# Opening laid out anew, and sum, squares and halves of two chunks moved to GpSimd

## Chip, cores and metric

One core of a Trainium2 chip. The metric is the device time of one execution, in microseconds. Engines by the names of the profile: PE is TensorE, DVE is VectorE, ACT is ScalarE, POOL is GpSimd, SP is the queue that issues most transfers.

## The reference

A conditioned transformer block on x of 8 batches by 256 tokens by 128 channels:

- condition: `sc = silu(c)`, `shift = sc @ shift_w.T + shift_b`, `scale = clip(sc @ scale_w.T + scale_b + 1, 0.1, 10)`
- `adaln(x) = x / max(norm(x) / sqrt(128), 1e-6) * norm_w * scale + shift`
- attention with 16 heads of 8 channels: softmax of `q k / sqrt(8)` with the keys whose mask value is 0 left out (a batch with no valid key gets equal weights), then times v, then the projection; `x = x + attention(adaln(x))`
- MLP: 128 to 1024 channels, halves `x1` and `x2`, `silu(x1) * x2`, 512 to 128; `x = x + mlp(adaln(x))`

## The kernel before

Channels lie on the partitions and tokens run along the row. The 2048 tokens are four chunks of 512 (two batches each). In the opening they come in five pieces (`PIECES`): pieces 0 and 1 are the two batches of chunk 0, pieces 2 to 4 are chunks 1 to 3.

**Opening, for each piece e.** ACT squares x (`square`), PE averages over the channels with a matmul against `mean_w` (`mean_square`), ACT takes a logarithm and an exponential (`inverse_norm`), DVE multiplies (`norm`), ACT applies gain and shift (`shifted`) and gives `h`. PE makes queries, keys and values from `h` (`q_or_k`, `values`). Queries and keys are cut into three bf16 parts: the first by ACT (`first_part_q`, `first_part_k`), the remainder by DVE (`rest_of_q`, `rest_of_k`), the rest by POOL (for piece 0 by DVE). Transfers lay the parts row by row into `q_stack` and `k_stack`, with rows for the mask and for the maxima.

**Attention.** A unit is a pair of heads of one batch, 64 units in all. The loop on PE runs over positions p = 0 to 71. At position p, PE makes the scores of unit p with queries on the partitions (`query_scores`, two banks of a ring of three), and of unit p - 8 with keys on the partitions (`key_scores`, another ring of three); at u = p - 8 it also multiplies exponentials by values (`p_times_v`). DVE takes the maxima of the first kind of scores, two reductions of a unit (`maxima`). After each four units (half a batch, index k) POOL cuts the maxima in two bf16 parts, PE turns them (`turn_maxima`, position 4k + 4), DVE copies them (`turned`) and POOL issues two transfers that put them into `q_stack`. ACT takes the exponentials of the second kind of scores. The ring of three banks holds scores, turned maxima, the projected chunk and its mean square in one order (`ITEMS`); a bank is written again once its last user has read it, and every engine works in program order.

**Between.** SP stores the outputs with their sums to DRAM and loads them back as `o_num` and `o_den`. When a chunk is complete, at fixed positions behind it (`P_...`), ACT takes the reciprocal of the sums, DVE multiplies (`over_sum`), PE projects (`project`), DVE adds x (`residual`), ACT squares (`square_2`), PE averages (`mean_square_2`), DVE applies the lower bound (`guard_2`), ACT makes the inverse norm, DVE multiplies in two halves (`norm_2`), ACT adds the shift and rounds to `h2_hi` (`shifted_2`), DVE makes the remainder `h2_lo` (`second_part_h2`). This is so for chunks 0 and 1; chunks 2 and 3 end in the MLP loop. Three times two instructions of POOL cut the MLP weights between k = 6 and k = 11 (L463, L466).

**MLP.** 16 steps of two three-part matmuls, a sigmoid, two multiplications and a three-part matmul back.

Positions that the change touches: `PRE_...` are positions p at which pieces 2 to 4 do their steps (PE: `PRE_SQUARE`, `PRE_Q`, `PRE_K`, `PRE_V`; DVE: `PRE_NORM`, `PRE_REST_Q`, `PRE_REST_K`). POOL works its loop over k at L429 to L466. The order on ACT in the opening is written out at L806 to L840, on PE at L686 to L697, on DVE at L1089 to L1106.

## Time and profile before

| | us |
|---|---|
| median of 3 runs | 187.12 |
| lowest, highest run | 186.57, 262.2 |
| profiled execution | 188.25 |
| its span, first to last instruction | 186.2 |

| engine | busy us | share of the span |
|---|---|---|
| PE | 150.3 | 81% |
| DVE | 147.9 | 79% |
| ACT | 136.3 | 73% |
| POOL | 75.5 | 41% |

The profiled execution's own time is 2.05 us more than its span. Sums below are made against the profiled execution. All times inside the trace are in us from the span's start. A line number such as L1032 is the line of the kernel that issued the instruction.

### The profile page before, as it was taken

To read this page: it belongs to the slowest core of one execution; us is meant where nothing else is said; L and a number is where in the kernel's file an instruction comes from. 1 tells how busy PE (TensorE), PEld (TensorE's weight loads), DVE (VectorE), ACT (ScalarE), POOL (GpSimd) and SP (SyncE) were. 2 spreads that over 40 slices of the span, in tenths; PEclk is the share of its full clock that TensorE was granted. 3 is DMA by queue.
4 is the path that set the end of the run, shared out by engine and by line. 5 is a ranking of instruction groups with operands and counts; after the bars stand their busy time and mean duration, and the time that the engine had idled before them with its cause. 6 is when DMAs were issued, how large, how long until landed. Compare 5 with 4: busy or idle time off the path is not lost.

```text
span 186.2 us, 3731 instructions
## 1 busy us (share of the span) xinstructions
PE 150.3 (81%) x1312; PEld 75.8 (41%) x1312; DVE 147.9 (79%) x258; ACT 136.3 (73%) x247; POOL 75.5 (41%) x125
## 2 busy tenths in 40 slices
PE   7772997649998898778867778877799994998992
PEld 7440543323333333223323322323223872785870
DVE  8675389875999999998999998999332956987993
ACT  7566265666778888957978856988988699689550
POOL 8249117975663133603423512302300252553750
PEclk9997599996999999999999999999999999999999
DMA  4846224427311373621112112112122110010103
GB/s 131 277 145 204 78 80 138 127 58 206 90 59 61 118 206 110 192 89 40 58 60 58 62 60 58 56 59 61 62 84 85 65 51 0 2 56 0 55 5 113
DMA packets 17512, 16.38 MB, mean 88 GB/s; under 512 B 2846, under 2 KB 16598, under 8 KB 17494
## 3 DMA queue, kind: packets, MB, share of 16 engines
q1 hardware_dynamic: 16086, 15.21, 26.5%
q0 software_dynamic: 1408, 0.93, 1.9%
q8 instruction: 11, 0.18, 0.4%
q14 instruction: 7, 0.06, 0.1%
HBM read 4.34 MB, written 5.24 MB: 51 GB/s over the span
## 4 chain that ended last, share of the span: by engine, by line
DVE 35%; PE 28%; issue 15%; DMA 7%; POOL 7%; SPq 3%; ACT 3%; DVEq 0%; POOLq 0%; ACTq 0%
DVE neg_max L1032 24%; PE bank L549 5%; POOL gated_lo L473 5%; PE bank L619 3%; PE bank L511 3%; ACT p_exp L882 2%; DMA mask_sb<-mask 2%; PE bank L601 2%; DMA o_rows<-o_sb 2%; PE bank L521 2%; PE bank L570 2%; DVE o_num L1053 2%; PE bank L575 2%; DMA o_den<-o_rows 2%; SPq L318 2%
## 5 line engine op out<-in xcount | busy, mean ns | idle before, releaser
L1032 DVE TENSOR_REDUCE neg_max<-bank 128x2 f32<-128x512 f32 x128 | 81.8, 686 | 12.0 <-PE bank L549 11.4
L882 ACT ACTIVATE p_exp<-bank 128x512 f32<-128x512 f32 x128 | 69.5, 598 | 20.5 <-PE bank L601 19.5
L619 PE MATMUL bank<-p_exp,v_all 128*9 128x256 f32 x512 | 40.0, 386 | 0.2
L549 PE MATMUL bank<-k_stack,q_stack 62*128 62x256 bf16 x256 | 26.3, 281 | 17.0 <-DVE neg_max L1032 11.7
L473 POOL TENSOR_TENSOR gated_lo<-rs,gated_hi 128x512 fp32r<-128x512 f32 x14 | 18.2, 1302 | 28.6 <-ACT gated_hi L906 27.6
L601 PE MATMUL bank<-q_stack,k_stack 64*128 64x256 bf16 x256 | 25.9, 274 | 3.9 <-DVE rest L997 2.0
L549 PEld LDWEIGHTS bank<-k_stack,q_stack 62*128 62x128 bf16 x256 | 8.9, 94 | 45.5 <-DVE neg_max L1032 36.1
L445 POOL DMA_DIRECT2D q_stack<-max_rows x32 | 17.6, 553 | 20.8 <-DVE max_rows L1041 20.8
L435 POOL CAST max_parts<-neg_max 128x16 bf16<-128x16 f32 x16 | 3.5, 220 | 47.2 <-DVE neg_max L1032 47.2
L601 PEld LDWEIGHTS bank<-q_stack,k_stack 64*128 64x128 bf16 x256 | 12.6, 96 | 10.3 <-ACT p_exp L882 4.1
L664 PE MATMUL bank<-h_hi,w_parts 128*128 128x512 f32 x32 | 13.0, 407 | 1.6 <-DVE rs L1155 1.4
L619 PEld LDWEIGHTS bank<-p_exp,v_all 128*9 128x9 f32 x512 | 7.7, 88 | 15.2 <-issue 8.6
L1147 DVE SCALAR_TENSOR_TENSOR xn<-bank,small_sb,h 128x512 f32<-128x512 f32 x16 | 11.9, 744 | 2.5 <-ACT h L913 2.5
L666 PE MATMUL bank<-h_hi,w_parts 128*128 128x512 f32 x32 | 12.5, 391 | 0.0
L665 PE MATMUL bank<-h_lo,w_parts 128*128 128x512 f32 x32 | 12.5, 390 | 0.0
L1155 DVE SCALAR_TENSOR_TENSOR rs<-bank,small_sb,xn 128x512 f32<-128x512 f32 x16 | 12.0, 751 | 0.6
L913 ACT ACTIVATE h<-bank,small_sb 128x512 f32<-128x512 f32 x16 | 10.9, 679 | 1.7 <-PE bank L666 1.6
L906 ACT ACTIVATE gated_hi<-rs 128x512 fp32r<-128x512 f32 x14 | 8.8, 629 | 4.0 <-DVE rs L1155 4.0
L511 PE MATMUL bank<-h,front 128*128 128x512 f32 (+1 forms) x20 | 8.9, 542 | 2.8 <-DVE rest L997 1.1
L419 POOL DMA_DIRECT2D k_stack<-parts x12 | 6.4, 541 | 5.8 <-ACT parts L792 5.8
L406 POOL TENSOR_TENSOR parts<-rest,parts 128x512 bf16<-128x512 f32 (+1 forms) x8 | 8.5, 1089 | 0.0
L846 ACT ACTIVATE o_sb<-bank 128x512 f32<-128x512 f32 x14 | 8.5, 606 | 0.0
(106 smaller groups left out, 214.1 us busy)
## 6 DMA issues: line engine op xcount, KB each, us to landing
o_rows<-o_sb SPq DMA_DIRECT2D x16, 256.0 KB, 2.1
q_stack<-parts SPq DMA_DIRECT2D x18, 128.0 KB
k_stack<-parts SPq DMA_DIRECT2D x18, 128.0 KB
o_num<-o_rows SPq DMA_DIRECT2D x8, 128.0 KB, 2.5
o_den<-o_rows SPq DMA_DIRECT2D x8, 128.0 KB, 3.4
out_t<-o_num SPq DMA_DIRECT2D x8, 128.0 KB, 2.0
back<-back_w SPq DMA_DIRECT2D x1, 832.0 KB, 7.7
x_sb<-x_t SPq DMA_DIRECT2D x3, 256.0 KB, 5.1
```

The costliest lines, as they stand in the source:

```text
L445: pool.dma_start(q_stack[first:first + 2, c % STACKS, q0:q0 + 4, at * N:(at + 1) * N], max_rows[G * r:G * (r + 1), k % 2, :]).then_inc(s_m ...
L473: nc.gpsimd.tensor_tensor(gated_lo[:, n % GB, :], gated[:, n % GB, :], gated_hi[:, n % GB, :].bitcast(F32), ALU.subtract).then_inc(s_gated ...
L511: nc.tensor.matmul(bank[:, QK_BANKS[e][i], at], qkv_w[:, i * C:(i + 1) * C], h[:, c % 2, at], start=True, stop=True).then_inc(s_qk, 1)
L549: mm = nc.tensor.matmul(scores[r][:, t * N:(t + 1) * N], q_stack[rows, c % STACKS, g, at + t * 128:at + (t + 1) * 128], k_stack[rows, c % ...
L601: mm = nc.tensor.matmul(bank[:, RING + (v + r) % RING, t * N:(t + 1) * N], k_stack[rows, c % STACKS, g, at + t * 128:at + (t + 1) * 128], ...
L619: mm = nc.tensor.matmul(bank[32 * j:32 * j + VW, 6 + k % 2, (q % 2) * N:(q % 2 + 1) * N], v_all[:, b, t, 2 * g + j, :], p_exp[:, (2 * q + ...
L664: nc.tensor.matmul(out, w_hi, h2_hi[:, c, :], start=True, stop=False)
L665: nc.tensor.matmul(out, w_hi, h2_lo[:, c, :], start=False, stop=False)
L666: nc.tensor.matmul(out, w_lo, h2_hi[:, c, :], start=False, stop=True).then_inc(s_w1, 1)
L882: nc.scalar.activation(p_exp[:, u % 4, par, :, :], bank[:, RING + v % RING, :].rearrange("p (t q) -> p t q", t=KT), ACT.Exp, scale=D ** -0 ...
L1032: nc.vector.tensor_reduce(out=neg_max[:, k % 2, :, par, g], in_=bank[:, n % RING, :].rearrange("p (t k) -> p t k", t=KT), axis=AX.X, op=AL ...
L1155: nc.vector.scalar_tensor_tensor(out=gated[:, n % GB, :], in0=bank[:, first + 1, :], scalar=b1, in1=silu[:, n % 2, :], op0=ALU.add, op1=AL ...
```

## The change

- SP issues the mask's transfer second, after the small vectors and ahead of `front_w` and the second piece of x.
- On PE the flags by channel come ahead of the second mean; the means of pieces 3 and 4 and the values of chunk 0 come ahead of the first scores. Banks are given out anew. On ACT the squares of pieces 3 and 4 and the inverse norms come earlier, the values of chunk 3 ahead of the last first parts. `PRE_...` positions are changed.
- For chunks 0 and 1 (`EARLY` = 2): `over_sum` and the squares go to POOL, at k = 4(c + 1) + 3 and + 4. `guard_2` goes: ACT takes the logarithm straight from the bank, with a small bias, and the bound is put on the inverse in `norm_whole`, one DVE instruction over the chunk. ACT applies gain and shift in two halves (`shifted_whole`) to an f32 `h2`; POOL makes `h2_hi` and `h2_lo` from it (`parts_h2`, at k = 4(c + 1) + 6).
- The projection stands one position later (11 for 10), its mean square one later (14 for 13), logarithm and exponential one earlier on ACT. These hold for all of chunks 0 to 2 where they apply.

```diff
-PRE_SQUARE = (-1, -1, -1, 1, 3)
-PRE_Q = (-1, -1, 2, 5, 8)
-PRE_K = (-1, -1, 3, 6, 8)
-PRE_V = (1, 4, 6, 8)
-PRE_NORM = (-1, -1, -1, 3, 6)
-PRE_REST_Q = (-1, -1, 4, 7, 9)
-PRE_REST_K = (-1, -1, 5, 7, 9)
+PRE_Q = (-1, -1, 1, 4, 8)
+PRE_K = (-1, -1, 2, 6, 8)
+PRE_V = (-1, 3, 5, 7)
+PRE_NORM = (-1, -1, -1, 0, 2)
+PRE_REST_Q = (-1, -1, 2, 5, 8)
+PRE_REST_K = (-1, -1, 3, 5, 9)
...
-    P_SECOND_PART = (7, 8, 9, 10, 12, 13, 15, 16, 17, 19, 22)
+    P_SECOND_PART = (7, 8, 9, 11, 12, 14, 14, 15, 17, 19, 22)
...
+EARLY = NC - 2
+K_OVER_SUM, K_SQUARE, K_PARTS_H2 = (3, 4, 6)
...
             sp.dma_start(small_sb[:, :], small).then_inc(s_in, 16)
+            sp.dma_start(mask_sb[:, :], mask).then_inc(s_in_mask, 16)
             sp.dma_start(front[:, :], front_w).then_inc(s_wa, 16)
             load_x(1)
-            sp.dma_start(mask_sb[:, :], mask).then_inc(s_in_mask, 16)
...
+            def over_sum(c):
+                pool.wait_ge(s_rec, 2 * c + 2)
+                nc.gpsimd.tensor_tensor(o_num[:, c, :], o_num[:, c, :], o_den[:, c, :], ALU.mult).then_inc(s_on, 1)
+
+            def square_2(c):
+                pool.wait_ge(s_ad, drained(item("project", c)))
+                nc.gpsimd.tensor_tensor(sq2[:, c % 2, :], y[:, c, :], y[:, c, :], ALU.mult).then_inc(s_sq2, 1)
+
+            def parts_h2(c):
+                pool.wait_ge(s_h2_whole, BC * (c + 1))
+                nc.gpsimd.tensor_copy(h2_hi[:, c, :], h2[:, c, :]).then_inc(s_h2_early, 1)
+                pool.wait_ge(s_h2_early, c + 1)
+                nc.gpsimd.tensor_tensor(h2_lo[:, c, :], h2[:, c, :], h2_hi[:, c, :].bitcast(F32),
+                                        ALU.subtract).then_inc(s_h2_lo_early, 1)
...
+                    if ITEMS[n - RING][0] == "square" and ITEMS[n - RING][1] < EARLY:
+                        pe.wait_ge(s_inv2, 2 * ITEMS[n - RING][1] + 1)
...
             scale_and_shift()
+            flags_by_channel()
             mean_square(1)
-            flags_by_channel()
             keep_clock(WARM[1])
-            for i in range(2):
-                q_or_k(0, i)
-            for i in range(2):
-                q_or_k(1, i)
+            query(0)
+            key(0)
+            query(1)
+            key(1)
             mean_square(2)
+            values(0)
+            mean_square(3)
+            mean_square(4)
...
             shifted(1)
+            square(3)
             first_part_q(1)
             first_part_k(1)
+            square(4)
             inverse_norm(2)
-            square(3)
-            shifted(2)
             values(0)
             inverse_norm(3)
-            square(4)
+            shifted(2)
+            inverse_norm(4)
+            shifted(3)
             first_part_q(2)
-            shifted(3)
             first_part_k(2)
-            inverse_norm(4)
             values(1)
+            shifted(4)
             first_part_q(3)
-            shifted(4)
             first_part_k(3)
             values(2)
+            values(3)
             first_part_q(4)
             first_part_k(4)
-            values(3)
...
+            def norm_whole(c):
+                dve.wait_ge(s_inv2, 2 * c + 2)
+                nc.vector.scalar_tensor_tensor(out=xn2[:, c, :], in0=rs2[:, c, :], scalar=1 / EPS, in1=y[:, c, :],
+                                               op0=ALU.min, op1=ALU.mult).then_inc(s_xn2, 1)
```

## Rows read from the trace of the kernel before

**Rows 1.** Page, part 1: busy us, share of the span, instructions of each engine.
```profile
PE 150.3 (81%) x1312; PEld 75.8 (41%) x1312; DVE 147.9 (79%) x258; ACT 136.3 (73%) x247; POOL 75.5 (41%) x125
```
**Rows 2.** Chain that ended last, in the opening: start, us, what.
```profile
2.59 4.37 DMA mask_sb<-mask
...
14.29 2.40 DMA q_stack<-parts
```
**Rows 3.** Timeline, 5 to 17 us: start, us, engine, line, operation, tiles, shapes.
```profile
5.58 0.17 DVE L954 TENSOR_TENSOR cond<-small_sb,sig 128x8 f32<-128x8 f32 x1
6.39 0.68 PE L503 MATMUL bank<-sq,mean_w 128*128 128x256 f32 x2
6.99 0.28 DVE L958 TENSOR_SCALAR valid<-mask_sb 8x256 f32<-8x256 int32 x1 [1.25 <-DMA mask_sb<-mask]
7.62 0.42 ACT L758 ACTIVATE rs<-rs 128x256 f32<-128x256 f32 x1
7.75 0.22 DVE L963 TENSOR_SCALAR any_diag<-eye,any_valid 8x8 f32<-8x8 f32 x1
8.89 0.42 DVE L989 SCALAR_TENSOR_TENSOR xn<-rs,x_sb 128x256 f32<-128x256 f32 x1
9.54 0.34 DVE L981 TENSOR_SCALAR mask_add<-valid,any_valid 8x256 bf16<-8x256 f32 x1
...
11.07 7.67 SPq L318 DMA_DIRECT2D q_stack<-parts  x12
```
**Rows 4.** Timeline, 12 to 22 us, means and values on PE.
```profile
12.89 1.02 PE L503 MATMUL bank<-sq,mean_w 128*128 128x512 f32 x2
...
18.65 2.07 PE L521 MATMUL bank<-front,h 128*128 128x128 f32 x8
```
**Rows 5.** Windows: stretch, us, busy us and instructions by engine, granted clock, DMA share, GB/s.
```profile
16.72:22.40 5.68, 4.89 (x20) 2.51 (x22) 2.58 (x4) 1.02 (x2) 2.64 (x5) 0.50 0.43 126
17.37:47.56 30.19, 24.07 (x148) 11.11 (x148) 22.94 (x40) 16.08 (x32) 16.60 (x24) 0.85 0.42 120
```
**Rows 6.** Timeline, 31 to 48 us: POOL, one wait of PE, one turn.
```profile
31.50 2.71 POOL L406 TENSOR_TENSOR parts<-rest,parts 128x512 bf16<-128x512 f32 x2
35.90 1.80 POOL L452 MEMSET q_stack<- 128x2048 uint32 x1
41.09 0.39 PE L601 MATMUL bank<-q_stack,k_stack 64*128 64x256 bf16 x4 [1.98 <-DVE rest L997]
47.56 0.27 DVE L1041 COPY max_rows<-bank 16x256 bf16<-16x256 bf16 x1
```
**Rows 7.** Windows between turns: three undisturbed ones, then four of chunk 0.
```profile
58.91:75.93 17.02, 15.00 (x198) 6.04 (x198) 15.80 (x28) 14.28 (x28) 5.16 (x13) 1.00 0.46 135
75.93:104.55 28.62, 21.94 (x268) 8.47 (x268) 26.36 (x45) 22.86 (x46) 9.87 (x20) 1.00 0.26 81
```
**Rows 8.** Timeline, 63 to 126 us: POOL's wait, chunk 0's steps, a later turn.
```profile
63.41 0.20 POOL L435 CAST max_parts<-neg_max 128x16 bf16<-128x16 f32 x1 [2.84 <-DVE neg_max L1032]
...
77.61 1.29 POOL L463 TENSOR_TENSOR w_parts<-back,w_parts 128x512 fp32r<-128x512 f32 x1
77.78 1.68 DVE L1053 TENSOR_TENSOR o_num<-o_num,o_den 128x512 f32<-128x512 f32 x1
80.74 0.75 DVE L1056 SCALAR_TENSOR_TENSOR rest<-bank,small_sb,x_sb 128x512 f32<-128x512 f32 x1
86.42 0.69 DVE L1062 TENSOR_SCALAR parts<-bank 128x512 f32<-128x512 f32 x1 [0.56 <-PE bank L575]
92.64 1.80 DVE L1068 SCALAR_TENSOR_TENSOR o_den<-rest,gain,parts 128x256 f32<-128x256 f32 x2
101.24 0.87 DVE L1078 SCALAR_TENSOR_TENSOR h_lo<-o_den,shift,h_hi 128x256 fp32r<-128x256 f32 x2
...
125.82 0.27 DVE L1041 COPY max_rows<-bank 16x256 bf16<-16x256 bf16 x1
```
**Rows 9.** Line L1053 alone: count, ns min/median/max, first and last start.
```profile
L1053 DVE TENSOR_TENSOR o_num<-o_num,o_den x4: 687/1184/1679, 77.8 to 154.1; 128x512 f32<-128x512 f32 x4
```

More of the change, by code:

```diff
@@ L135, in item, with drained @@
     return ITEMS.index(what)
+def drained(n):
+    return sum(not (what[0] == "square" and what[1] < EARLY) for what in ITEMS[:n + 1])
 def build(nc, x_t, small, mask, front_w, back_w, out_t):
@@ L453, in _ @@
                       .then_inc(s_fill_q[2], 1)
+                for c in range(EARLY):
+                    if k == 4 * (c + 1) + K_OVER_SUM:
+                        over_sum(c)
+                    if k == 4 * (c + 1) + K_SQUARE:
+                        square_2(c)
+                    if k == 4 * (c + 1) + K_PARTS_H2:
+                        parts_h2(c)
                 if 6 <= k < 12:
@@ L871, in shifted_2, with shifted_whole @@
                     at = (b % BC) * N
-                    act.wait_ge(s_xn2, b + 1)
+                    act.wait_ge(s_xn2, EARLY + b - BC * EARLY + 1)
                     nc.scalar.activation(h2_hi[:, c, at:at + N], xn2[:, c, at:at + N], ACT.Identity,
                                          bias=shift[:, b:b + 1]).then_inc(s_h2, 1)
+            def shifted_whole(c):
+                if c == 0:
+                    act.wait_ge(s_stack[NP - 1], 16 * STACK_DMAS)
+                act.wait_ge(s_xn2, c + 1)
+                for i in range(BC):
+                    b = BC * c + i
+                    at = slice(i * N, (i + 1) * N)
+                    nc.scalar.activation(h2[:, c, at], xn2[:, c, at], ACT.Identity,
+                                         bias=shift[:, b:b + 1], scale=gain[:, b:b + 1]).then_inc(s_h2_whole, 1)
             for u in range(UNITS):
@@ L1122, in _ @@
                     behind = p - LEAD - BC * G * (c + 1)
-                    if behind == P_OVER_SUM:
+                    if c >= EARLY and behind == P_OVER_SUM:
                         over_sum(c)
@@ L1135, in _ @@
                         guard_2(c, n % RING, s_ad)
-                    if c < NC - 2 and behind == P_NORM:
-                        norm_2(c)
-                    if c < NC - 2 and behind == P_SECOND_PART:
-                        second_part_h2(c)
+                    if c < EARLY and behind == P_NORM:
+                        norm_whole(c)
             drain_output(HALVES - 1)
```

118 lines of the change are left out of this document (74 added, 44 removed).

## The prediction

> **What bounds the kernel now.** I read the busy shares first. PE and DVE are both near 80% [rows 1]; no engine is full on average, so the stages have different limits, and I went on to the chain of waits, the timeline of each stage and the windows between landmarks.
>
> In the opening the chain runs over the mask's transfer, the mask's arithmetic on DVE, SP's own queue and the landing of the query parts [rows 2]: the first scores start at 14.29 + 2.40 = 16.7. From there to the third turn of the maxima at 47.56, DVE works 22.94 of 30.19 us and is idle for 7.25 [rows 5, 6]; PE is at the lower of its two levels (granted 0.50, 1.2 GHz) from 16.72 to 22.40, after it had stood still since 13.91, the end of the third mean [rows 4, 5]. So here order and waits cost more than work.
>
> From about 59 on, the loop is DVE's: three undisturbed periods of four units take 17.02 us, 5.67 each, with DVE busy for 15.80 of them; its idle 0.41 per period is the wait after each turn [rows 7]. PE (15.00) and ACT (14.28) are close behind, so DVE work removed is gained only as far as these two follow. The steps of chunk 0 lengthen four periods to 28.62, which is 28.62 - 4 x 5.67 = 5.94 us more [rows 7]. Chunk 1 repeats this between 104.55 and 125.82: 21.27 - 17.02 = 4.25, and one more `second_part_h2` of 0.87 in the last period, 5.12 in all [rows 7, 8].
>
> **Up to the first scores: 0 expected, the start 0.3 later.** The mask would be there by 5.75, when DVE is through with the condition (5.58 + 0.17); its price of landing second isn't in the trace, but it need only beat 5.75 in place of 6.96. Then the flags end 0.98 after that start as now (6.99 to 7.97) [rows 3], at about 6.75. But the flags' matmul now stands ahead of the second mean on PE. That mean started at 6.39 and moves to about 7.2, its 0.68 ends at 7.9, the inverse norm behind it on ACT (it ended at 7.62 + 0.42 = 8.04, 1.65 after the mean began) ends at 8.85. `norm(1)` waits for it and began at 8.89 before: no gain. `mask_add` stands behind `norm(1)` on DVE and SP's mask rows behind `mask_add`, 9.88 now and about 9.85 then; the six query transfers of batch 0 follow at 11.07, as now, because SP's queue and not the data sets them [rows 3]. Whether `front_w` lands one issue later (some 0.4 us) matters only past 5.75. What is gained on the mask is thus given back by the mean: ends of the range here -0.6 and +0.3.
>
> PE gets three more blocks before the first scores: values of chunk 0 (8 pieces, 2.07 at the lower level, so half, 1.04, at the full one) and two means of 1.02 [rows 4]. From 13.91 that makes 13.91 + 3.08 = 17.0 against 16.7: the first scores 0.3 late. At the low level they'd take 6.2 and end at 20.1; PE works right up to them, so I take the high level.
>
> **From the first scores to the third turn: 2.5 less.** What was spread over p = 1 to 3 on PE at the lower level (values, two means) is gone from there, and the normalisations are three to four positions earlier. I walked the positions in order, with each engine's program order and these prices: 1.25 to 1.3 for a unit's two reductions (15.80 less three copies of 0.27, over 12 units), 0.4 for a scores block, 1.1 for a query, key or mean (1.02 and the hand-over), 1.05 for values, 0.42 for an activation of 256 columns [rows 3, 4, 6, 7]. DVE runs nearly through from p = 0 to 5, with three waits left:
> - At p = 5 DVE wants the remainder of the keys of piece 3, but PE makes those keys at p = 6, behind values of chunk 2 (1.05), scores (0.4), key (1.1), and ACT copies them (2 x 0.42): 3.4 after the scores of p = 5, of which two reductions and the query's remainder hide 1.9. Idle 1.5 to 1.6.
> - At p = 8 the turn stands behind scores, key scores, query and key of piece 4: 0.4 + 0.4 + 2.2 + 0.3 = 3.3, DVE has its reductions until 1.75. Idle 1.6. POOL's fills (two of 1.80) and parts (2.71) end about 0.6 before that turn [rows 6], so they are covered; without the query and key there, POOL would set it.
> - `zero_outputs` at p = 10 waits for the last remainder: 0.4.
>
> With about 1.5 in bubbles of 0.1 to 0.4 that is 5.1 idle for 7.25. `norm(3)` no longer meets POOL's subtraction: 0.5 less of work. PE's wait of 1.98 for the last remainder at p = 9 goes [rows 6]. Sum: 17.4 + 0.2 + 22.4 + 5.1 = 45.1 for the third turn that was at 47.56: **2.5 us**. Bounds: nothing, if each wait removed is replaced; 6, if only the bubbles of 1.5 stay. I keep the walk's value.
>
> **Chunks 0 and 1: 3.3 less.** Now per chunk [rows 8]: `over_sum` 1.68 on DVE and residual 0.75; an idle 0.56 for the mean and the bound 0.69; `norm_2` 1.80; `second_part_h2` 0.87. These are 6.35, and 5.94 shows in the periods, so 0.1 of each of the four goes into slack: 2.33, 1.15, 1.70, 0.77. After:
> - `over_sum` on POOL costs DVE nothing, 1.29 on POOL by its nearest row, the subtraction of L463. That starts 1.68 after the turn at 75.93, behind its transfers, and ends at 78.9; the projection, now at p = 35, comes at 79.9 (75.93, 0.25 to the next scores, two units of 1.25, and 1.2 for scores, key scores and values). But the projection's 1.1 was hidden by the reductions that DVE did after `over_sum`; now DVE waits 0.7 for it and adds 0.75. With 0.1 less of other idle: 1.36 in that period for 2.33 before.
> - Square on POOL: k = 8, behind turn 8 and its transfers, 1.29 long. By the walk it ends 0.55 after PE arrives at the mean of p = 38. PE waits with all behind it: scores of p = 39 come 1.1 + 0.55 late, less 0.2 of slack: 1.45, against 1.15 now. A loss of 0.3. The bank waits for ACT's logarithm, which comes right behind the mean and isn't late for p = 40.
> - `norm_whole` 0.7 uncovered, 1.6 if it meets POOL's subtraction as `norm_2` does at p = 41 (same position): chunk 0 1.55 for 1.70; chunk 1, where POOL has nothing then, 0.56.
> - `second_part_h2` goes to POOL (k = 10 and 14; 1.29 and a rounding, at most as much again): all of it saved. ACT has two squares less.
>
> Chunk 0: 0.97 - 0.3 + 0.15 + 0.77 = 1.6; chunk 1: 5.12 - 1.36 - 1.45 - 0.56 = 1.75. **3.3 us** together; bounds 1.5 (each POOL step late by 0.5 once a chunk) and 5.5 (no projection wait, no late square).
>
> What POOL covers: its idle per undisturbed period is 2.84 [rows 8]. The fullest new periods (k = 7, 11: 2 x 1.29; k = 10: 1.29 and two roundings, estimated at half of it each) need 2.6, just under it. If that cover is gone, each later turn comes late by the excess.
>
> Rows against a rule: `over_sum` takes 0.69 to 1.68 for one form [rows 9], and the long one ran while POOL's subtraction ran, 77.61 to 78.90, and ended 0.56 after it [rows 8]. The Trainium skill (SBUF — State Buffer, "SBUF: two separate sides") says that DVE with two SBUF inputs and a GpSimd operation reading SBUF exclude each other, whoever starts first holding the ports; the trace agrees. By that rule more POOL work speaks against the change, yet DVE's reductions and residual take their main input from PSUM, so the only new meeting is `norm_whole`; the sum would be the same within 0.9.
>
> **Tail and MLP: 0.** Chunk 2's projection and mean go one position on, 1.1 each in a stretch where ACT's exponentials set the pace; whether they come at 66 and 69 or 67 and 70 changes which exponential waits, not how many. The bound on chunk 2 still ends before PE needs it. Within 0.5 either way.
>
> **Sum.** -2.5 - 3.3 = -5.8 against 188.25 of the profiled execution, 182.4. That execution is 1.1 above the median of the runs, 187.12; there it gives 181.3.
>
> **The rivals.**
> 1. The opening gives nothing: a key made after its reader (p = 5) and a late turn eat it. For it: both waits are new and visible in the positions. Only the 3.3 stays: 187.1 - 3.3 = 183.8, down to 185.6 with the low bound. Chance 0.20.
> 2. The opening gains near its bound: DVE's idle falls to the bubbles, and the square isn't late (PE arrives later than I place it). 6 + 4 less: 177; middle of this case 178.5. Against it: the order of p = 5. Chance 0.17.
> 3. Slower: POOL becomes the pace of the turns. Place: the six new steps at k = 7, 8, 10, 11, 12, 14, each waiting for another engine with the next turn's parts queued behind. Price: an operation of 1.29 stretched or waiting; the slack is 0.25 in k = 7, 10, 11. It turns the sign when the six together cost over 5.8, nearly 1 us each; at 1.6 each it is 187.1 - 5.8 + 9.6 = 190.9. Against it: POOL is idle for most of the rest, and the DVE steps that could hold its ports are gone. Chance 0.04 for over 2%.
> 4. The change doesn't do what it says at the mask: the mask isn't on the path once the mean is behind it. This is in my forecast already.
>
> **How the numbers follow.** Forecast case 0.59, own range 179.5 to 183.4; predicted 181.3. 2%, 3.7 us, is about what a measurement of this kernel tells from no change: faster means below 183.4. Faster: 0.59 less a small part at its edge, and 0.17: 0.74. Within 2%: rival 1, that edge and mild forms of rival 3: 0.22. Slower 0.04. The range leaves out the far ends: 178.0 to 184.8.
>
> **What would show it.** First scores at 16.7 to 17.1 and mask rows on SP near 9.9; clock at the full level from 14 to 23; DVE idle before the remainder L1007's counterpart at p = 5 for 1.5; third turn near 45; chunk 0's four periods 27.0 instead of 28.6; PE waiting for POOL's square at p = 38 by 0.5; reductions in runs without a gap elsewhere. I am wrong if the mask rows start over 0.5 earlier, if the turns after k = 7 wait for POOL, or if ACT and not DVE sets the periods without chunk work.

## The result and the profile after

The changed kernel takes 181.47 us (median of 4 runs, 180.69 to 183.31) against 187.97 for the kernel before in the same comparison: ratio 0.967, 95% interval 0.959 to 0.975. It is faster. The forecast was 181.3 in 178.0 to 184.8. One run of the kernel before took 262.2; the ratio leaves it out, and without it that kernel's median is 187.12 and the difference 5.7. The profiled execution took 180.74 (span 178.8), 7.5 less than the profiled execution before with its 188.25.

"PE's level" below is the clock granted to it: the upper level is a granted 1.00 (2.4 GHz), the lower one 0.50 (1.2 GHz).

The busy shares of the changed kernel, which answer to [rows 1]:

```profile
PE 146.9 (82%) x1312; PEld 75.7 (42%) x1312; DVE 141.4 (79%) x248; ACT 134.7 (75%) x245; POOL 83.1 (46%) x133
```

DVE has 6.5 us less work and POOL 7.6 more. Where the 7.5 us came from is read off the turns of the maxima, a mark that both traces have 16 times:

| | before | after | gained |
|---|---|---|---|
| first scores | 16.73 | 17.94 | -1.2 |
| third turn | 47.56 | 43.89 | 3.7 |
| eighth turn, start of chunk 0's steps | 75.93 | 72.27 | 3.7 |
| twelfth turn, end of them | 104.55 | 98.92 | 5.6 |
| fifteenth turn, end of chunk 1's steps | 125.82 | 118.88 | 6.9 |
| sixteenth turn | 132.01 | 124.41 | 7.6 |
| from there to the execution's own time | 56.24 | 56.33 | -0.1 |

So in these two executions the opening gave 3.7 us, the chunks 3.9, tail and MLP nothing.

**Opening.** The timeline of the changed kernel up to the first scores answers to [rows 3]. L1033 and L1056 are the flags and `mask_add`, L529 the small matmuls of `keep_clock`, L331 the query transfers, L609 the scores:

```profile
5.66 0.42 DVE L1033 TENSOR_SCALAR valid<-mask_sb 8x256 f32<-8x256 int32 x1
7.81 2.77 PE L529 MATMUL bank<-mean_w 128*128 128x128 f32 x12
9.66 0.34 DVE L1056 TENSOR_SCALAR mask_add<-valid,any_valid 8x256 bf16<-8x256 f32 x1
11.78 6.45 SPq L331 DMA_DIRECT2D q_stack<-parts  x10
17.94 0.40 PE L609 MATMUL bank<-k_stack,q_stack 62*128 62x256 bf16 x4 [0.53 <-DMA q_stack<-parts]
```

The flags start at 5.66 instead of 6.99, but `mask_add` at 9.66 instead of 9.54: the early mask brings nothing here, as forecast. The twelve small matmuls take 2.77; before they took 1.60. PE was at its lower level, the first query began at 10.37, and the query transfers at 11.78 instead of 11.07.

Windows of the changed kernel: the stretch of the small matmuls, first scores to third turn (without the first 0.4; [rows 5] leaves out the first 0.6), an undisturbed stretch of three periods, chunk 0 [rows 7]. Columns as in [rows 5].

```profile
7.80:10.60 2.80, 2.80 (x14) 2.79 (x13) 0.96 (x3) 1.90 (x4) 0.00 (x0) 0.50 0.80 311
18.36:43.89 25.53, 18.12 (x136) 7.98 (x136) 21.94 (x39) 14.63 (x30) 15.78 (x24) 1.00 0.45 127
55.24:72.27 17.03, 15.08 (x198) 6.07 (x198) 15.81 (x29) 14.31 (x29) 5.16 (x13) 1.00 0.48 142
72.27:98.92 26.65, 21.76 (x268) 8.61 (x268) 23.33 (x39) 21.78 (x44) 13.95 (x24) 1.00 0.26 83
```

The undisturbed stretch is the same to 0.01 us. Between first scores and third turn DVE's idle time fell from 7.25 to 25.53 - 21.94 = 3.6, its work by 1.0. Chunk 0 fell from 28.62 to 26.65, chunk 1 from 21.27 to 19.96 and by 0.7 more in the period behind it.

The stretch from first scores to third turn is not the same in every execution of this order. Windows from the first to the second turn, of the changed kernel and of `norm_18` below, which differs from it only behind the eighth turn:

```profile
26.98:36.87 9.89, 7.06 (x46) 3.83 (x48) 6.78 (x14) 2.73 (x6) 8.37 (x10) 1.00 0.30 84
```

```profile
27.76:39.15 11.39, 8.56 (x46) 4.93 (x48) 6.77 (x13) 2.73 (x6) 8.38 (x10) 0.85 0.28 78
```

The work is the same, and 1.5 us hang on one fall of PE's level (at 33.1 to 37.1 in `norm_18`). Of the six executions of the change's order up to that turn (the change, `open_only`, `flags_behind`, `fb_nokeep`, `norm_18`, `blocks_late`), only the change's own had no such fall; the other five took 11.3 to 11.5 there. First scores to third turn is 25.95 in the change and 27.4 to 27.5 in `open_only`, `flags_behind`, `fb_nokeep` and `norm_18`. So about 1.5 of the opening's 3.7 us hang on the change's execution having met no fall; the profiled one of before met one in the next period, which took 8.74 at a granted 0.80, where the change's took 7.02.

The timeline of the changed kernel on DVE between the first turn (26.98) and the third; L1082 is the remainder of the keys of piece 3, turns are L1116, and the bracket is the idle time before:

```profile
31.06 0.88 DVE L1082 SCALAR_TENSOR_TENSOR rest<-bank,any_all,parts 128x256 f32<-128x256 f32 x2 [1.54 <-ACT parts L855]
36.87 0.28 DVE L1116 COPY max_rows<-bank 16x256 bf16<-16x256 bf16 x1 [0.99 <-PE bank L620]
```

Timeline of the changed kernel, chunk 0's steps, which answer to [rows 8]. L1131 is the residual, L434 POOL's square, L635 the mean over it, L1107 the reductions, L463 POOL's wait for the maxima, L1141 `norm_whole`:

```profile
77.26 0.75 DVE L1131 SCALAR_TENSOR_TENSOR rest<-bank,small_sb,x_sb 128x512 f32<-128x512 f32 x1 [0.56 <-PE bank L630]
80.83 1.05 POOL L434 TENSOR_TENSOR sq<-rest 128x512 f32<-128x512 f32 x1
82.03 1.10 PE L635 MATMUL bank<-sq,mean_w 128*128 128x512 f32 x2 [0.22 <-POOL sq L434]
83.48 2.61 DVE L1107 TENSOR_REDUCE neg_max<-bank 128x2 f32<-128x512 f32 x4 [1.17 <-PE bank L609]
84.84 0.20 POOL L463 CAST max_parts<-neg_max 128x16 bf16<-128x16 f32 x1 [2.41 <-DVE neg_max L1107]
87.72 1.28 POOL L499 TENSOR_TENSOR w_parts<-back,w_parts 128x512 fp32r<-128x512 f32 x1
87.86 1.70 DVE L1141 SCALAR_TENSOR_TENSOR o_den<-parts,rest 128x512 f32<-128x512 f32 x1
```

POOL still has 2.41 us to spare at that turn. DVE waits 0.56 for the projection, PE waits 0.22 for the square, DVE 1.17 behind that mean, and `norm_whole` runs into POOL's subtraction and takes 1.70.

### The profile page after: what moved, and what is told of

The parts are those of the page before. It is cut to its first block, busy times and chain, and to the rows that moved or that the text cites. A ratio compares the mean times of both kernels' runs of the same rounds, so it can differ in the third digit from the quotient of the medians.

```text
span 178.8 us, 3725 instructions
## 1 busy us (share of the span) xinstructions
PE 146.9 (82%) x1312; PEld 75.7 (42%) x1312; DVE 141.4 (79%) x248; ACT 134.7 (75%) x245; POOL 83.1 (46%) x133
## 4 chain that ended last, share of the span: by engine, by line
DVE 35%; PE 29%; issue 15%; ACT 10%; POOL 8%; DMA 2%; DVEq 0%; POOLq 0%; ACTq 0%
DVE neg_max L1107 24%; ACT p_exp L959 5%; POOL gated_lo L509 5%; PE bank L679 5%; PE bank L609 5%; PE bank L661 2%; DMA q_stack<-max_rows 2%; PE bank L635 2%; PE bank L630 2%; PE bank L564 2%; PE bank L728 2%; PE bank L529 1%; PE bank L553 1%; DVE rest L1082 1%; DVE k_stack L1017 1%
## 5 line engine op out<-in xcount | busy, mean ns | idle before, releaser
L1107 DVE TENSOR_REDUCE neg_max<-bank 128x2 f32<-128x512 f32 x128 | 81.5, 686 | 9.2 <-PE bank L609 8.8
L959 ACT ACTIVATE p_exp<-bank 128x512 f32<-128x512 f32 x128 | 69.8, 603 | 15.7 <-PE bank L661 14.6
L679 PE MATMUL bank<-p_exp,v_all 128*9 128x256 f32 x512 | 39.5, 381 | 0.3
L609 PE MATMUL bank<-k_stack,q_stack 62*128 62x256 bf16 x256 | 25.2, 271 | 17.2 <-DVE neg_max L1107 14.0
L661 PE MATMUL bank<-q_stack,k_stack 64*128 64x256 bf16 x256 | 25.3, 270 | 3.6 <-ACT p_exp L959 3.0
L609 PEld LDWEIGHTS bank<-k_stack,q_stack 62*128 62x128 bf16 x256 | 8.9, 93 | 43.4 <-DVE neg_max L1107 38.7
L463 POOL CAST max_parts<-neg_max 128x16 bf16<-128x16 f32 x16 | 3.1, 195 | 29.5 <-DVE neg_max L1107 29.5
L728 PEld LDWEIGHTS bank<-h_hi,w_parts 128*128 128x128 f32 x32 | 6.0, 187 | 5.2 <-DVE rs L1233 2.2
```

The lines of the kernel that those rows point to most:

```text
L609: mm = nc.tensor.matmul(scores[r][:, t * N:(t + 1) * N], q_stack[rows, c % STACKS, g, at + t * 128:at + (t + 1) * 128], k_stack[rows, c % ...
L661: mm = nc.tensor.matmul(bank[:, RING + (v + r) % RING, t * N:(t + 1) * N], k_stack[rows, c % STACKS, g, at + t * 128:at + (t + 1) * 128], ...
L679: mm = nc.tensor.matmul(bank[32 * j:32 * j + VW, 6 + k % 2, (q % 2) * N:(q % 2 + 1) * N], v_all[:, b, t, 2 * g + j, :], p_exp[:, (2 * q + ...
L728: nc.tensor.matmul(out, w_hi, h2_hi[:, c, :], start=True, stop=False)
L959: nc.scalar.activation(p_exp[:, u % 4, par, :, :], bank[:, RING + v % RING, :].rearrange("p (t q) -> p t q", t=KT), ACT.Exp, scale=D ** -0 ...
L1107: nc.vector.tensor_reduce(out=neg_max[:, k % 2, :, par, g], in_=bank[:, n % RING, :].rearrange("p (t k) -> p t k", t=KT), axis=AX.X, op=AL ...
```

## The experiments

Each time is a median with its range, and the ratio is to the kernel before, run beside it on the same chip. Times inside a trace come from one execution of each kernel. The first four kernels shared one chip, the next four a second, the last four a third; the kernel before took 187.97, 189.3, 190.22 and 189.18 in the four comparisons, so kernels of different comparisons are held together by their ratios.

### The two halves apart

`open_only` is the kernel before with the opening's part of the change (mask, orders on PE and ACT, banks, `PRE_...`); `chunk_only` has the chunks' part (steps on POOL, `norm_whole`, `P_...`). Both diffs are cut to their core.

```diff
 open_only, against the kernel before
-PRE_K = (-1, -1, 3, 6, 8)
+PRE_K = (-1, -1, 2, 6, 8)
...
+            values(0)
+            mean_square(3)
+            mean_square(4)
 chunk_only, against the kernel before
+EARLY = NC - 2
+K_OVER_SUM, K_SQUARE, K_PARTS_H2 = (3, 4, 6)
```

> The kernel before with the opening of the changed kernel alone; the steps of chunks 0 and 1 stay on DVE and ACT. Theory: the two halves of the change are independent and add up, because the opening ends at the third turn and the chunk steps begin after the seventh. The trace of the changed kernel puts the third turn 3.67 us earlier (47.56 to 43.89), so this run is 3.7 us faster than before (2%), with the third turn at 43.9. Forecast of the prediction for this half: 2.5. Rival: the opening's gain is lost again behind it, where POOL and SP now meet the same transfers earlier: then the third turn is early, but the seventh is not (before 75.93), and the run is under 1 us faster.

> The kernel before with the steps of chunks 0 and 1 moved as in the changed kernel; the opening stays as before. Theory: 75.93 to 125.82 shrinks by 3.3, and the last period by 0.8: 4.0 us faster than before. Forecast of the prediction: 3.3. Rival: part of the chunks' gain needs the opening's earlier turns (POOL would be too full otherwise): then the turns after the seventh wait for POOL, and it is under 2.5 us.

`open_only`: 185.76 us (184.81 to 187.54), ratio 0.984, interval 0.974 to 0.993. First scores at 17.62, third turn at 45.00, and the periods of chunk 0 are 7.99, 6.86, 8.26 and 6.09, before 8.00, 6.86, 7.35 and 6.41. The third turn was expected at 43.9 and came 1.1 later: the fall of PE's level told of above took 1.4, and the start gave 0.3 back. Behind it a part of the gain was lost again in this execution, as the rival had it: the third turn is 2.6 earlier than before, the eighth 2.0, the sixteenth 1.4. One period took 6.58 for 5.67, with PE waiting 1.13 for the transfer of turned maxima into `q_stack`, and the one of 8.26 had a granted clock of 0.79. Its profiled execution, 187.54, is the slowest of its four. `chunk_only`: 185.42 us (184.16 to 186.11), ratio 0.980, interval 0.972 to 0.987. From first scores to third turn it takes 30.90 (before: 30.83), and chunk 0, window of `chunk_only`:

```profile
74.90:101.53 26.63, 21.76 (x268) 8.60 (x268) 23.32 (x39) 21.78 (x43) 13.97 (x24) 1.00 0.27 87
```

That is the changed kernel's 26.65 without its opening. The two ratios multiply to 0.964, against 0.967 for both together: each half is worth about 2% (1.6 and 2.0), and within their intervals they add up.

`chunk_only` also shows the opening with PE's old order and an early mask. In its profiled execution the flags started at 5.66 too, though the mask's transfer stands where it stood. Its timeline:

```profile
7.25 1.60 PE L528 MATMUL bank<-mean_w 128*128 128x128 f32 x12
9.07 1.07 SPq L323 DMA_DIRECT2D k_stack<-mask_add  x2
15.66 0.61 PE L587 MATMUL bank<-k_stack,q_stack 62*128 62x256 bf16 x4 [2.90 <-DMA q_stack<-parts]
```

With the mask early and the mean ahead of the flags, the mask rows go at 9.07 and the scores start at 15.66, 1.1 before those of the kernel before.

### The flags behind the second mean

```diff
             scale_and_shift()
-            flags_by_channel()
             mean_square(1)
+            flags_by_channel()
             keep_clock(WARM[1])
```

> The changed kernel with the flags' matmul put back behind the second mean on PE; the mask's transfer stays second. Theory of the prediction: the flags hold the second mean up by 0.8, and that alone eats what the early mask brings; without it the mean is at 6.4, norm(1) at about 8.1 and the mask rows 0.8 earlier on SP (9.2 for 10.08), the first scores up to 0.8 earlier. Rival, from the trace of the changed kernel: the granted clock falls at 7.8 there to 0.50, 12 small matmuls that keep the clock then take 2.77 in place of 1.60 and stand ahead of the first query; if the clock falls here too, the query and the first scores stay where they are (query 10.37, scores 17.9) whatever the mean does.

183.17 us (182.31 to 185.0), ratio 0.970, interval 0.961 to 0.979: no gain over the change. Its timeline:

```profile
8.38 2.93 PE L529 MATMUL bank<-mean_w 128*128 128x128 f32 x12
...
18.73 0.39 PE L609 MATMUL bank<-k_stack,q_stack 62*128 62x256 bf16 x4
```

The small matmuls took 2.93, after 2.77 in the change, and pushed the query to 11.11. So this run doesn't price the flags' place: PE's level decided, as the rival had it. Its price comes from executions whose small matmuls took 1.50 to 1.60: with the order of the change, `best` and `blocks_late` below start their scores at 16.66 and 16.67; with the old order, `chunk_only` at 15.66. The flags' place gives back 1.0, which is what the early mask brings where PE is at its upper level. In `flags_behind`, `norm_18` and `open_only` PE went from its three added blocks straight into the scores (18.73, 18.72, 17.62) with no wait for the transfer: there the blocks set the start, as the forecast's walk had it.

### The keys of piece 3 one position earlier

```diff
-PRE_K = (-1, -1, 2, 6, 8)
+PRE_K = (-1, -1, 2, 5, 8)
```

> The changed kernel with the keys of piece 3 made on PE at position 5 in place of 6. Theory of the prediction: DVE's wait of 1.54 before the keys' remainder at position 5 (31.06) comes from the keys being ordered behind their reader. Made at 5 they come before the scores of position 6, the wait shrinks to about 0.3, and the third turn comes up to 1.2 earlier. Rival: POOL sets the second turn (its fills end at 35.5), so DVE's time is lost again there and the third turn moves by less than 0.5.

183.19 us (178.91 to 184.5), too spread for an interval; the run of 178.91 had a mean granted clock of 0.998, the others 0.962 to 0.990. The wait of 1.54 is gone, and the next turn waits 2.00 in place of 0.99. First the changed kernel's cast of the maxima, then `key3_early`'s, its turn on PE and the copy behind it:

```profile
35.51 0.19 POOL L463 CAST max_parts<-neg_max 128x16 bf16<-128x16 f32 x1
```

```profile
36.18 0.19 POOL L463 CAST max_parts<-neg_max 128x16 bf16<-128x16 f32 x1
36.81 0.27 PE L620 MATMUL bank<-ident,max_parts 128*16 128x128 bf16 x2 [0.95 <-POOL max_parts L465]
37.12 0.28 DVE L1116 COPY max_rows<-bank 16x256 bf16<-16x256 bf16 x1 [2.00 <-PE bank L620]
```

From the first turn to that cast it is 8.54 in both (26.98 to 35.51, 27.64 to 36.18). In the change PE starts the turn at 36.55, behind query and key of piece 4, when POOL has been through with the maxima for 0.55. In `key3_early` PE is there earlier and waits 0.95 for POOL, which has the parts and two fills ahead of its cast. So the second turn comes 9.48 after the first, 0.4 sooner than in the change, not 1.5. The next one came 8.35 later, for 7.02, at a granted clock of 0.80: this execution met its fall of the level there, and from the first scores the third turn is 0.9 later than in the change.

### POOL's fills ahead of everything

`key3_early` with the two fills (`memset` of the third buffers of `k_stack` and `q_stack`) moved from behind the first turn to the front of POOL's work.

```diff
+            nc.gpsimd.memset(k_stack[:, 2, :, :]..., ONES_BF16).then_inc(s_fill_k[2], 1)
+            nc.gpsimd.memset(q_stack[:, 2, :, :]..., 0).then_inc(s_fill_q[2], 1)
             for j in range(3):
...
-                if k == 0:
-                    ... the same two
```

> The changed kernel with the two fills of the third stack buffers (1.80 each on POOL) moved from behind the first turn to POOL's idle stretch at the start (6.0 to 12.6), and the keys of piece 3 made at position 5. Theory from key3_early: making the keys earlier took away DVE's wait of 1.54, but the second turn still came 8.5 after the first as POOL was busy with transfers, parts and fills until then, so DVE waited 2.0 there. With the fills gone from that place POOL is free at about 5 after the first turn and the second turn comes about 8.3 after the first in place of 9.5 to 9.9, the third 1.2 to 1.8 earlier counted from the first scores (25.95 to about 24.4); the run is 1 to 1.5 us faster than the changed kernel. Rival: query and key of piece 4, which stand ahead of that turn on PE, set it anyway: then it gains under 0.5.

185.62 us (184.05 to 188.71), ratio 0.975, interval 0.956 to 0.994. Later on it does what it should: second turn 8.46 after the first. But the start lost 4 us. The timeline of `fills_first`, and the one line of the changed kernel to hold beside it:

```profile
4.45 4.95 DVE L1024 TENSOR_SCALAR sig<-sig 128x8 f32<-128x8 f32 x1
...
7.58 1.79 POOL L452 MEMSET q_stack<- 128x2048 uint32 x1
9.98 0.57 PE L517 MATMUL bank<-cond,front 128*128 128x8 f32 x2 [4.35 <-DVE cond L1028]
```

```profile
4.45 0.85 DVE L1025 TENSOR_SCALAR sig<-sig 128x8 f32<-128x8 f32 x1
```

One addition over eight columns on DVE took 4.95 instead of 0.85 and ended at 9.40, just behind POOL's last fill (7.58 + 1.79 = 9.37). The condition hangs on that addition, and the scores started at 22.65. The fills are the only thing that was moved against `key3_early`, so moving them cost this; that they held the addition is read from the two ends that coincide. How is open: the first fill is recorded from 5.77, when the addition is usually over (5.30).

### The flags behind and no small matmuls

```diff
             mean_square(1)
-            keep_clock(WARM[1])
+            flags_by_channel()
             query(0)
```

> The changed kernel with the flags' matmul behind the second mean, and without the six small matmuls that keep the clock ahead of the first query. Theory: in flags_behind h was ready at 9.4, the query started at 11.1 since the small matmuls took 2.93 at the lower level; without them the query starts when h is ready (8.5 to 9.4) and the first scores come 1.2 to 2.5 earlier than 17.9, so 15.7 to 16.7. Rival: without them PE stays at the lower level longer, queries, means and values take twice as long (3.1 more for the blocks ahead of the first scores), and the first scores come no earlier than 17.9.

184.56 us (183.86 to 187.56), ratio 0.973, interval 0.960 to 0.986. Its window of 7 to 17.4 us and its timeline:

```profile
7.00:17.40 10.40, 8.16 (x22) 5.63 (x22) 5.93 (x19) 6.70 (x14) 5.98 (x11) 0.53 0.72 227
```

```profile
13.51 1.91 PE L541 MATMUL bank<-sq,mean_w 128*128 128x512 f32 x2
```

The query started at 8.51, as soon as `h` was there, but without the small matmuls the level was the lower one nearly throughout (granted 0.53 in the window), a mean took 1.91 instead of 1.02, and the scores started at 19.19. In `flags_behind`, whose small matmuls were slow too, the means were back at 1.02 and the scores came at 18.73. So in these traces the small matmuls bring the level back ahead of the means; the two ratios, 0.973 and 0.970, do not tell the kernels apart. At the upper level they take 1.5 us of PE.

### `norm_whole` one position later

```diff
-                    if c < EARLY and behind == P_NORM:
+                    if c < EARLY and behind == P_NORM + 1:
                         norm_whole(c)
```

> The changed kernel with norm_whole one position later (42 and 58 in place of 41 and 57). Theory: its 1.70 in chunk 0 is DVE waiting while POOL's subtraction (two inputs in SBUF) runs; one position later that is over, and the instruction takes 0.68 as in chunk 1; the period from the tenth to the eleventh turn of the maxima shrinks from 7.24 to 6.2, one us in all. Rival: the length comes from the data or from ACT's shift next to it, then it stays near 1.7.

181.69 us (179.3 to 181.92), ratio 0.957, interval 0.943 to 0.970. Its timeline:

```profile
90.03 1.29 POOL L499 TENSOR_TENSOR w_parts<-back,w_parts 128x512 fp32r<-128x512 f32 x1
91.43 0.68 DVE L1141 SCALAR_TENSOR_TENSOR o_den<-parts,rest 128x512 f32<-128x512 f32 x1
```

Started 0.11 behind POOL's subtraction instead of 0.14 into it, the same instruction takes 0.68 for 1.70, and that period 6.22 for 7.24: 1.0 us for one line moved. The ratio alone doesn't show it, its interval holds the change's 0.967. By the exclusion that the prediction quoted from the Trainium skill (SBUF — State Buffer, "SBUF: two separate sides") the meeting costs POOL's rest, here 87.72 + 1.28 - 87.86 = 1.14 of the 1.28; measured 1.02, so it holds. The same section has it that a one-input form of DVE is shut out too when it runs in a mode with both ports, and then by any GpSimd operation; that may be what held the addition in `fills_first`, but no run here tells that cause from another.

### The three blocks behind the first scores

```diff
             mean_square(2)
-            values(0)
-            mean_square(3)
-            mean_square(4)
...
                     query_scores(p)
+                if p == 0:
+                    values(0)
+                    mean_square(3)
+                    mean_square(4)
```

> The changed kernel with values of chunk 0 and the means of pieces 3 and 4 put back behind the first scores on PE (position 0). Theory of the prediction: they gain by filling the stretch in which PE waits for the first scores, and by keeping its clock; moved back, PE stands still for some 2.5 us ahead of the first scores, the granted clock falls to 0.50 about when they start as in the kernel before, the three blocks take 4 to 6 us at that level with DVE waiting, and the third turn comes 3 to 5 us later counted from the first scores (25.95 to 29 or more). Rival: the gain is in the earlier normalisations and not in these blocks; then it is under 1.5 later.

187.97 us (185.67 to 188.87) beside 190.22 of the kernel before, too spread for an interval. Its timeline, and its window from the first scores to the first turn:

```profile
16.67 0.61 PE L609 MATMUL bank<-k_stack,q_stack 62*128 62x256 bf16 x4 [3.08 <-DMA q_stack<-parts]
17.21 2.07 PE L578 MATMUL bank<-front,h 128*128 128x128 f32 x8
19.07 3.59 PE L541 MATMUL bank<-sq,mean_w 128*128 128x512 f32 x4
```

```profile
16.67:30.47 13.80, 11.89 (x48) 5.44 (x48) 8.77 (x15) 8.47 (x16) 2.97 (x7) 0.79 0.34 95
```

PE stands still for 3.08 ahead of the scores, its granted clock falls, and the same three blocks take 5.7 instead of the 2.9 that they take at the upper level. First scores to first turn is 13.80, against 9.04 in the change: 4.8 us for blocks of 2.9, and as much as was expected (3 to 5). First scores to third turn is 32.24, against 25.95 in the change and 30.83 before; the other 1.5 of that difference is the fall between first and second turn (11.41), which `norm_18` has with the blocks in their place, so it isn't the blocks'. The opening's gain hangs on these three blocks: they fill the stand-still before the scores, where PE is free, and PE's level stays up for what comes behind.

### The mask alone

`mask_second` is the kernel before with the mask's transfer second; `mask_flags` has the flags ahead of the second mean as well.

```diff
             sp.dma_start(small_sb[:, :], small).then_inc(s_in, 16)
+            sp.dma_start(mask_sb[:, :], mask).then_inc(s_in_mask, 16)
...
 mask_flags also:
-            mean_square(1)
             flags_by_channel()
+            mean_square(1)
```

> The kernel before with the mask's transfer second and nothing else. The trace of chunk_only, whose opening is that of the kernel before, had the mask there by 5.66 in that execution (6.96 in the kernel before), mask rows on SP at 9.07 and first scores at 15.66 for 16.73. Theory: with the second mean where it was, an early mask is worth that 1.0: mask rows at 9.1 and first scores at 15.7 when PE is at its upper level by 5.9, later by what the small matmuls take at the lower level (2.8 for 1.6). In the time at most 1.0 (0.5%). Prediction: a mask second alone would be worth up to 0.6 before the first scores. Rival: the first scores hang on the parts of batch 0 and SP's queue, and stay at 16.7.

> The same, and the flags' matmul ahead of the second mean on PE as in the changed kernel. Theory of the prediction: the mean starts at 7.2 in place of 6.3, the mask rows come at 9.9 to 10.1, the first scores at 16.5 to 16.8 with PE at its upper level: the flags' place gives back what the mask brings. Rival: no difference to mask_second.

`mask_second`: 192.14 us (191.46 to 192.64) beside 189.18, ratio 1.023, interval 1.015 to 1.031. `mask_flags`: 191.3 us (189.58 to 192.52), ratio 1.017, interval 1.007 to 1.027. Both are slower than before. Their mean granted clock was 0.937 to 0.964; five runs of the kernel before at 0.946 to 0.955 took 189.9 to 191.0 themselves, so a part of the loss goes with the level. Timelines of `mask_second`, then of `mask_flags`:

```profile
17.99 0.61 PE L549 MATMUL bank<-k_stack,q_stack 62*128 62x256 bf16 x4 [3.14 <-DMA q_stack<-parts]
...
77.93 0.63 ACT L754 ACTIVATE o_den<-o_den 128x512 f32<-128x512 f32 x1 [1.79 <-DMA o_den<-o_rows]
```

```profile
18.67 0.40 PE L549 MATMUL bank<-k_stack,q_stack 62*128 62x256 bf16 x4 [2.72 <-DMA q_stack<-parts]
```

In both the twelve small matmuls took long (2.56 and 2.77, for 1.60 before), and the scores started 1.3 and 1.9 later than before; between the two, the flags' place costs 0.7. `mask_second` lost 1.6 more in the first period of chunk 0 (9.62 for 8.00), where ACT's reciprocal waited 1.79 for `o_den` and PE 1.39 for ACT behind it. `mask_flags` lost 3.9 in three later periods (6.74, 7.58 and 8.31 for 5.67, 5.67 and 7.35).

The expected 15.7 for `mask_second` was not reached, and these two runs show no gain from the early mask; the 1.1 of `chunk_only`, where the mask landed early by itself and PE had its upper level, is the only trace that does. Over all profiled executions, the twelve small matmuls took 1.60 in the two whose mask is issued late (before, `chunk_only`). With the mask second they took 1.50 in three (`best`, `best_gap`, `blocks_late`) and 2.29 to 2.93 in eight. Whether the order of the transfers has a part in this, the runs don't tell.

### A version that takes what these runs point to

`best` is the change with three edits: `PRE_K` as in `key3_early`; POOL's two fills behind the transfers of chunk 0's stacks, after the opening's conditions are done and before the first turn; `norm_whole` as in `norm_18`. `best_gap` has two more small matmuls ahead of `scale_and_shift()`.

```diff
-PRE_K = (-1, -1, 2, 6, 8)
+PRE_K = (-1, -1, 2, 5, 8)
...
                 first_k_stack(1, j)
+            nc.gpsimd.memset(k_stack[:, 2, :, :]..., ONES_BF16).then_inc(s_fill_k[2], 1)
+            nc.gpsimd.memset(q_stack[:, 2, :, :]..., 0).then_inc(s_fill_q[2], 1)
             for k in range(HALVES):
...
-                    if c < EARLY and behind == P_NORM:
+                    if c < EARLY and behind == P_NORM + 1:
 best_gap also:
             mean_square(0)
+            keep_clock(2)
             scale_and_shift()
```

> The changed kernel with three edits: norm_whole one position later, keys of piece 3 at position 5, and the two fills of the third stack buffers behind POOL's transfers for chunk 0 (about 20.5 to 24), where POOL waits 4.7 for the first maxima, and not in its first stretch, where DVE's short operations waited for them (4.95 for 0.85 in fills_first). Theory: first to second turn 8.5 for 9.9 (as in fills_first), norm_whole 0.68 for 1.70 (as in norm_18): 2.4 us less than the changed kernel in all, ratio to before about 0.955. Rival 1: the fills block DVE's normalisation at 23 (two inputs in SBUF) or delay POOL's first parts of the maxima; then 0.7 of it is lost. Rival 2: a fall of PE's clock around 40 to 47, as in key3_early and fills_first, eats 1.2 of it.

> The same with two more small matmuls between the first mean and the scale and shift matmuls, where PE stands still for 0.9. Theory: PE's level around 6 to 11 differs from execution to execution (twelve small matmuls take 1.5 or 2.8); with the pause filled it is at the upper level more often, and the mean granted clock of the runs is higher and the median up to 1 us lower. Rival: the two come at the lower level, delay the conditions by 0.5, and nothing else changes: 0.3 to 0.5 slower than without them.

`best`: **178.33 us** (6 runs, 177.13 to 179.62), ratio 0.951, interval 0.944 to 0.957, the lowest ratio here (that of `norm_18` overlaps it). `best_gap`: 179.46 us (177.81 to 181.81), ratio 0.954, interval 0.947 to 0.961: the two extra matmuls gave nothing, and the mean granted clock of its runs was not higher (0.971 to 0.998, for 0.981 to 1.0 in `best`). The timeline of `best`:

```profile
16.66 0.39 PE L608 MATMUL bank<-k_stack,q_stack 62*128 62x256 bf16 x4 [0.47 <-DMA q_stack<-parts]
...
20.95 1.83 POOL L459 MEMSET q_stack<- 128x2048 uint32 x1
22.15 0.68 DVE L1063 SCALAR_TENSOR_TENSOR xn<-rs,x_sb 128x512 f32<-128x512 f32 x1
35.36 0.28 DVE L1115 COPY max_rows<-bank 16x256 bf16<-16x256 bf16 x1 [0.99 <-PE bank L619]
87.59 0.68 DVE L1140 SCALAR_TENSOR_TENSOR o_den<-parts,rest 128x512 f32<-128x512 f32 x1
```

With the fills over by 20.95 + 1.83 = 22.78, POOL is free when the second turn comes: 8.13 after the first. `norm_whole` takes 0.68. A normalisation of two SBUF inputs beside a fill (22.15) takes its 0.68 too: the fill did not hold it. The first turn comes late here. The window of `best` up to it, and those of `best_gap` up to it and from it to the second turn:

```profile
16.66:27.23 10.57, 9.34 (x38) 3.94 (x40) 8.93 (x16) 6.44 (x14) 6.53 (x9) 0.68 0.49 138
```

```profile
16.66:25.71 9.05, 6.36 (x36) 2.57 (x36) 8.63 (x16) 6.83 (x14) 6.54 (x9) 1.00 0.57 162
25.71:34.18 8.47, 6.86 (x46) 3.91 (x48) 6.77 (x14) 2.84 (x6) 4.94 (x8) 1.00 0.35 99
```

The same work takes 10.57 at a granted 0.68 and 9.05 at 1.00. The change has it in 26.98 - 17.94 = 9.04. So `best`'s profiled execution lost 1.5 there to the level, and some work of the next period was done by then: its 8.13 can't be held against the change's 9.89. `best_gap` can, with its first turn at 9.05: 8.47 for 9.89, and the 1.4 is what `key3_early` had moved into another wait. From first scores to third turn it is 25.95 in the change, 25.72 in `best` and 24.54 in `best_gap`. With the 1.0 of the norm the edits give 2.4, as expected.

## Why the prediction was right, point by point

The total was right (181.47 for 181.3) and faster, and both halves gave somewhat more than forecast: forecast 2.5 and 3.3, by the traces 3.7 and 3.9, by the two kernels alone 1.6% and 2.0%. The gain between the profiled executions is 7.5, between the medians of one comparison 6.5, or 5.7 without the run of 262.2; the forecast was 5.8. That the time fell within 0.2 is in part luck: the start lost 0.9 more than forecast, the stretch behind it gained 2.1 more, and the profiled execution of the change is one of the two shorter ones of its four (180.7 at a mean granted clock of 0.989, the others 182.19 and 183.31 at 0.971).

**First scores: 0.3 later expected, 1.2 measured; the step failed.** The mask's part held: flags ahead of the second mean give back what the mask brings. "SP's queue and not the data sets them" did not: with PE at the lower level the data came later and the six query transfers went at 11.78, not at 11.07. The low bound of that level was put only on the three blocks (20.1), not on the matmuls ahead of the query, which are where it struck: 2.77 for 1.60. Where the level is the upper one, the start is 16.66, just under the forecast's 16.7 to 17.1; the three blocks then fit ahead of the scores with 0.47 to spare, and the forecast 0.3 was not needed.

**First scores to third turn: the mechanism was right, the size 2.1 too small** (25.95; the walk had 45.1 - 17.0 = 28.1). The wait for piece 3's keys was 1.54, forecast 1.5 to 1.6. The turn at p = 8 waited 0.99 for 1.6, `zero_outputs` 0.28 for 0.4, and the bubbles came to 0.8 for 1.5: 3.6 in all for 5.1, and DVE's work was 0.5 lower than in the walk. That POOL would be through about 0.6 before that turn held (0.55), and `key3_early` shows how thin that cover was: PE got there earlier, with query and key in place, and had to wait for POOL. Not foreseen was how much of the gain is the level: the clock was expected up from 14 to 23 and was (1.00 from 17.94 to the third turn, for 0.85 before), `blocks_late` shows 4.8 us hanging on it and on the order together, and a fall of the level between first and second turn, which the walk doesn't have, brings the stretch to 27.4 to 27.5 in four other kernels with this order, 0.6 to 0.7 under the walk.

**Chunks: 3.3 expected, 3.9 measured.** The projection's period was 6.86 (forecast 5.67 + 1.36 = 7.03), the mean's 6.88 (7.12), the normalisation's 7.24 (7.22), the last 5.67. The mean came in lower because POOL's square takes 1.05, not the 1.29 of its nearest row, and so PE waited 0.22, not 0.55. Chunk 1 repeats it (6.86, 6.88, 6.22). `norm_whole`'s meeting with POOL's subtraction was priced to 0.1 (1.70 for 1.6).

**POOL's cover** held: in every period from k = 7 on, POOL waited for DVE's maxima and not the other way about, 0.31 at the least (k = 7, 10 and 11, where the forecast had 0.25) and 2.41 at the turn shown. Rival 3 is out.

**Tail and MLP: 0 expected, 0.1 measured.**

**The rivals.** Rival 1 is excluded by `open_only` (interval below 1). Rival 2 named the right places, but did not hold: DVE's idle time fell to 3.6 and not to the bubbles, the three waits of the forecast are all there, and the square was still 0.22 late. The 178.33 of `best`, near its middle of 178.5, took three further edits.

**Open:** which level PE gets in the first 13 us. The change's profiled execution had the lower one there, the profiled one of before the upper one, `best` the upper one, and the order of PE's work at that place is the same in `best` and the change. Open too is why a fall of the level comes between first and second turn in some executions: with the keys of piece 3 at position 5 (`key3_early`, `fills_first`, `best`, `best_gap`) none of four had it there, though two of them (`key3_early`, `fills_first`) had one in the next period.

## What to carry to other kernels

Work put into a stand-still ahead of the first dependent block can be worth more than its own time, since PE's level may be kept for what follows (here 4.8 us for blocks of 2.9). Before you remove a wait, look up what sets the next turn once it is gone: here POOL's cast, which the fills held up, so the fills had to move in the same edit. When you put work on GpSimd, price it twice: what its queue delays, and which DVE instruction of two SBUF inputs runs at the same moment; moving that one by one position gave 1.0 here, beside 3.9 for the whole move. And before you put a difference between two traces down to an edit, compare the granted clock of the same stretch in both: one fall of it is 1.5 us here.

## What the runs showed of the hardware

- **The granted-clock record and the matmuls can disagree in the first 13 us.** In the changed kernel the record reads 0.50 there, as the matmuls do. In `flags_behind` the record says 1.00 from 8 to 12 us, and the twelve small matmuls take 2.93, near twice the 1.50 of `best` and no less than the 2.77 that the change has at a recorded 0.50. `norm_18`, `key3_early` and `mask_flags` take 2.77 at a recorded 1.00 as well. In that stretch the durations are what to read. The window of `flags_behind`:

```profile
8.00:12.00 4.00, 4.00 (x17) 3.80 (x18) 1.12 (x4) 1.87 (x4) 0.00 (x0) 1.00 0.59 219
```

- **The runs of one kernel spread with the level.** `key3_early` took 178.91 at a mean granted clock of 0.998 and 184.5 at 0.962; the change itself 180.7 at 0.989 (twice) and 183.31 at 0.971; five of `best`'s six runs were at 0.999 or 1.0. A part of `best`'s lead is that its runs met the upper level; whether its edits have a part in that isn't shown. What the traces give to them is 1.0 for the norm and 9.89 - 8.47 = 1.4 for the second turn.
- **With two fills at the front of GpSimd's work a small DVE instruction ended only when the last of them did** (4.95 for 0.85, in one execution), while a DVE instruction with two SBUF inputs ran beside a fill unhindered (0.68).
- **A GpSimd multiplication of 512 columns** took 1.05 with one tile as both inputs and 1.28 to 1.29 with two different ones.
